# Two groups of four heads per TensorE step in a five-part cross-attention stack

## The chip, the cores and the metric

One of the eight cores of a Trainium2 chip runs the whole program. The metric is the device time of one execution in microseconds, the median over runs. A profiled execution gives the trace: a start and a duration for each instruction of TensorE (PE for its matmuls, PEld for its weight loads), VectorE (DVE), ScalarE (ACT), GpSimd (POOL) and of the DMA queue of SyncE (SP).

## What is computed

16 sequences of 128 tokens with 128 channels pass through five attentions (parts L0, L1, L2, L3S, L3C). L0 has 8 heads, the others 16 heads of 8 channels. Cut to what matters:

```python
x = x + attention(layernorm(x), layernorm(ctx), heads=8)                    # L0
x = x + attention(x, ctx, heads=16, mask=causal & key_padding)              # L1
x = x + attention(x, ctx, heads=16) @ Wo + bo                               # L2
x = x + gelu(x @ W1 + b1) @ W2 + b2
x = layer_norm(x + attention(x, x, heads=16, mask=causal * pad) @ Wo1 + bo1)      # L3S
x = layer_norm(x + attention(x, ctx, heads=16, mask=pad) @ Wo2 + bo2)             # L3C
x = layer_norm(x + gelu(x @ W1 + bf1) @ W2 + bf2)
# attention: softmax(q k^T / sqrt(head channels)) v for each head, with float32 results
```

## The kernel before

**Units and positions.** A unit is two sequences (b = 0, 1) of one part: 8 units a part, 40 in all. Each unit has 8 positions of its own (`SLOT`), and `schedule()` puts every step of every unit at a position, before or behind its own first one: projections about three units ahead (`PREPARE`), the scores one unit ahead (`SCORE_AT`), the feed-forward work up to four units behind (`CHAIN`). Within a position `RANK` sets the order. All five engines walk the one list `STEPS` in order and do their share of each step, with semaphores between them, so no engine overtakes in the list.

**A group** is four heads of one sequence. A unit of L1 to L3C has eight groups, one at each position; a unit of L0 has four, one at every second position. For each group:

- `score`: queries times keys, 128x512, to one of two banks `score_ps`. VectorE takes the negated row maxima from it (line 745, `score_reduced`). Only these are used of it. When the four groups of a sequence are done, `nmax` splits the maxima into bf16 terms, `n_tr` transposes them and SyncE writes them into the operand `pairs` (`max_landed`).
- `attn`: keys times queries, transposed, with the maxima as further contraction rows, to one of two banks `attn_ps`; ScalarE takes the exponential (line 645, `exp_done`) into a ring of 5 buffers `probs`. In L1 GpSimd then zeroes what lies ahead of the diagonal (step `causal`, line 533).
- `pv`: probabilities times values, into the one bank `o_ps`, one or two positions after `attn` (`PV_AFTER`). After a sequence's last `pv`, ScalarE copies the bank out (`o_evac`, `o_saved`), `o_tr` transposes it, VectorE divides it into `attn_tok`, and `a_tr` transposes that back.

**The shapes on TensorE.** Masks (`diagonal`, line 816) are four 32x32 tiles: 32 rows, 32 columns. The `score` and `attn` matmuls of 16 heads contract 52 or 55 rows that begin at partition 0 for even units and at 64 for odd ones, half of the rows each; from L1 on the `attn` of unit u and the `score` of unit u+1 are issued in turn, four pairs of them, and lie in the two halves of the array at once (call them pairs). `pv` uses all 128 rows and 32 columns a head, four heads beside each other; float32 is two passes, so a group has eight matmul records. All else (projections, transposes, feed-forward; the steps in `MISC`) uses the whole 128x128 array and writes three banks `misc_ps` in turn, which VectorE or ScalarE empties (`evacuated`). L1 masks its scores; L3S masks its scores and its `attn`; L2 and L3C mask nothing.

**The order at a position before.** `attn` has rank -2 and comes first, with its masks and pairs; the transposes and small projections follow; `pv` of two positions ago has rank 25; `a_tr`, `wo` and the feed-forward have rank 30. On VectorE the reduction (`score`) has rank 2. TensorE's waits ahead of a group's matmuls are: the group two before reduced (`score_reduced`), the group two before exponentiated (`exp_done`), and for the first of a sequence `max_landed`.

Of the kernel before, what the change touches and what calls it, by code (L numbers as in the profile page):

```python
# [31 lines left out]
P = 128  # L32
BATCHES, S, D, FF = 16, 128, 128, 512
PAIR = 2
# [14 lines left out]
PROBS_RING = 5  # L49
# [26 lines left out]
    L1: (("qk", -25), ("split", -25), ("rest", -24), ("term1", -23), ("term2", -22), ("v", -13)),  # L76
    L2: (("qk", -25), ("split", -25), ("rest", -24), ("term1", -23), ("term2", -22), ("v", -11)),
    L3S: (("qk", -25), ("split", -25), ("rest", -24), ("term1", -23), ("term2", -22), ("v", -14)),
    L3C: (("qk", -25), ("split", -25), ("rest", -24), ("term1", -23), ("term2", -22), ("v", -13)),
# [4 lines left out]
PV_AFTER = {L0: 1, L1: 2, L2: 2, L3S: 2, L3C: 2}  # L84
O_TR_AFTER = {L0: 1, L1: 1, L2: 1, L3S: 1, L3C: 1}
CHAIN = {
    L0: (("a_tr", 10),),
    L1: (("a_tr", 13),),
    L2: (("a_tr", 12), ("wo", 13), ("w1", 15), ("w1", 15), ("square", 17), ("square", 18), ("cube", 18),
         ("cube", 19), ("tanh", 21), ("tanh", 21), ("gelu", 21), ("gelu", 22), ("w2_first", 25), ("w2", 26)),  # L90
    L3S: (("a_tr", 11), ("wo", 13), ("x_tr", 16), ("x_stats", 18), ("x_norm", 19), ("x_back", 22)),
    L3C: (("a_tr", 11), ("wo", 13), ("x_tr", 14), ("x_stats", 15), ("x_norm", 17), ("x_back", 19), ("w1", 21),
          ("w1", 21), ("w2_first", 23), ("w2", 24), ("x_tr", 27), ("x_stats", 28), ("x_norm", 30), ("out", 30),
          ("store", 30)),
# [3 lines left out]
RANK = {"attn": -2, "causal": 4, "w2": 17, "score": 2, "nmax": 11, "n_tr": 15, "o_tr": 16, "load": 20, "ln_in": 20,  # L98
        "raw_tr": 20, "ln_norm": 14, "ln_tr": 2, "qk": 20, "split": 20, "rest": 20, "term1": 20, "term2": 20,
        "v": 20, "mask": 20, "stack": 20, "pv": 25, "o_evac": 2, "a_tr": 30, "wo": 30, "w1": 30, "square": 14,  # L100
# [14 lines left out]
def schedule():  # L115
# [6 lines left out]
    for u in range(UNITS):  # L122
        part = u // SETS
        quads = HEADS[part] // QUAD
        every = 4 // quads
# [4 lines left out]
        for b in range(PAIR):  # L130
            for g in range(quads):
                pos = 4 * b + every * g
# [5 lines left out]
            last = 4 * b + every * (quads - 1)  # L138
# [51 lines left out]
def build(nc, x, ctx_in, weights, cols, rows, valid, valid_t, pad, pad_t, out):  # L190
    with ExitStack() as stack:
# [55 lines left out]
        attn_tok = sb("attn_tok", [P, PAIR, D])  # L247
# [410 lines left out]
        def _(dve):  # L658
            for step in STEPS:
# [103 lines left out]
                if kind == "o_tr":  # L763
# [4 lines left out]
                    dst = attn_tok[:, b, :].rearrange("p (h e) -> p h e", e=d)  # L768
# [36 lines left out]
        def _(pe):  # L805
# [47 lines left out]

            for step in STEPS:
# [60 lines left out]
                if kind == "attn":  # L915
# [4 lines left out]
                    if beside:  # L920
                        score_begins(beside)
                    if g == 0:

                        pe.wait_ge(max_landed[m % 4], (m // 4 + 1) * 16)
# [135 lines left out]
```

## Time and profile before

| | us |
|---|---|
| median of 3 runs | 562.75 (554.84 to 569.61) |
| profiled execution | 558.87 |
| its span, first to last instruction | 557.1 |
| granted TensorE clock, mean | 0.932 |

The first `attn` group of each part is exponentiated at 42 us (L0), 131 us (L1), 233 us (L2), 334 us (L3S) and 432 us (L3C); the last group of all near 532 us. The clock column of a window is the share of 2.4 GHz that was granted in it on the mean; the clock has two levels, 1.2 and 2.4 GHz. Busy time of PE counts overlapping matmuls once and is modelled at its end, so the start times of successive matmuls tell more of its speed than its busy share does.

### The profile page before, as it was taken

The numbers are of one execution on the slowest core, as the hardware profiler recorded it, in microseconds if no ns is written. First come the engines' busy times: TensorE is split into PE (matmuls) and PEld (weight loads), VectorE is DVE, ScalarE is ACT, GpSimd is POOL, SyncE is SP. The second block draws the span as 40 slices with busy tenths as digits, with TensorE's granted clock in tenths as the row PEclk, the third lists the DMA queues.
The fourth block names the chain that finished last, engine by engine and source line by source line (L and its number), as shares of the span: only waits on it lengthen the run. The fifth ranks groups of instructions, "written<-read, shape, count | busy, mean of one in ns | idle before, by whom it ended". The sixth has DMA issues, their size and how long they took to land.

```text
span 557.1 us, 16733 instructions
## 1 busy us (share of the span) xinstructions
PE 486.3 (87%) x6464; PEld 299.2 (54%) x6464; DVE 407.6 (73%) x1093; ACT 329.0 (59%) x662; POOL 263.4 (47%) x334
## 2 busy tenths in 40 slices
PE   1548876799999878899999999999999999999973
PEld 1436554455555544455666666565555556666652
DVE  6267876645688886687888877778878897788452
ACT  1424655433556554467777766656666767888851
POOL 3585776824666774524344433334333533422243
PEclk9977889965799996799999999999999999999998
DMA  4593323332233332232223322232333332220000
GB/s 112 99 274 100 103 60 96 81 72 62 64 68 86 76 78 54 59 77 69 69 67 69 69 62 60 54 70 63 77 69 85 80 79 60 69 62 14 13 20 19
DMA packets 72021, 40.68 MB, mean 73 GB/s; under 512 B 7016, under 2 KB 71560, under 8 KB 71816
## 3 DMA queue, kind: packets, MB, share of 16 engines
q1 hardware_dynamic: 71944, 39.61, 30.1%
q8 instruction: 53, 0.87, 0.7%
q14 instruction: 24, 0.20, 0.1%
HBM read 5.00 MB, written 1.05 MB: 11 GB/s over the span
## 4 chain that ended last, share of the span: by engine, by line
PE 65%; POOL 9%; ACT 7%; DVE 6%; SPq 5%; issue 4%; DMA 3%; POOLq 0%; ACTq 0%; DVEq 0%
PE o_ps L963 14%; PE attn_ps L933 12%; PE misc_ps L993 5%; PE misc_ps L984 5%; PE misc_ps L895 5%; PE misc_ps L970 4%; PE misc_ps L901 4%; PE misc_ps L896 3%; PE score_ps L816 3%; PE misc_ps L980 2%; POOL probs L533 2%; PE misc_ps L976 2%; POOL rest L521 2%; PE misc_ps L912 2%; POOL terms L523 2%
## 5 line engine op out<-in xcount | busy, mean ns | idle before, releaser
L745 DVE TENSOR_REDUCE max_words<-score_ps 128x4 f32<-128x512 f32 x288 | 195.8, 685 | 67.7 <-PE score_ps L849 66.1
L645 ACT ACTIVATE probs<-attn_ps 128x512 f32<-128x512 f32 x288 | 169.8, 596 | 110.5 <-PE attn_ps L933 107.2
L963 PE MATMUL o_ps<-probs,v 128*32 128x128 f32 x2304 | 127.0, 294 | 12.6 <-POOL probs L533 8.0
L849 PE MATMUL score_ps<-pairs 52*128 52x128 bf16 (+1 forms) x1152 | 118.7, 226 | 9.1 <-DMA pairs<-terms 9.1
L521 POOL TENSOR_TENSOR rest<-qk_f,terms 128x512 f32<-128x512 f32 x40 | 46.2, 1155 | 162.3 <-ACT terms L596 162.3
L933 PE MATMUL attn_ps<-pairs 55*128 55x128 bf16 (+1 forms) x1152 | 117.8, 225 | 1.9 <-issue 1.0
L933 PEld LDWEIGHTS attn_ps<-pairs 55*128 55x128 bf16 (+1 forms) x1152 | 66.7, 97 | 49.9 <-issue 34.1
L963 PEld LDWEIGHTS o_ps<-probs,v 128*32 128x32 f32 x2304 | 46.3, 110 | 60.0 <-issue 16.9
L849 PEld LDWEIGHTS score_ps<-pairs 52*128 52x128 bf16 (+1 forms) x1152 | 69.8, 98 | 11.0 <-DMA pairs<-terms 9.5
L533 POOL TENSOR_SCALAR_AFFINE_SELECT probs<-probs 128x512 f32<-128x512 f32 x64 | 39.9, 635 | 22.4 <-ACT probs L645 22.4
L527 POOL TENSOR_TENSOR terms<-rest,terms 128x512 bf16<-128x512 f32 x40 | 46.8, 1170 | 1.9
L654 ACT ACTIVATE o_sb<-o_ps 128x256 f32<-128x256 f32 x80 | 30.9, 386 | 27.8 <-PE o_ps L963 27.6
L523 POOL TENSOR_TENSOR terms<-qk_f,terms 128x512 bf16<-128x512 f32 x40 | 46.1, 1153 | 0.0
L970 PE MATMUL misc_ps<-ident,o_sb 128*128 128x128 f32 x160 | 35.0, 302 | 9.8 <-ACT o_sb L654 9.0
L513 POOL TENSOR_SCALAR var_eps<-mean_var 128x2 f32<-128x2 f32 (+1 forms) x32 | 7.1, 222 | 75.7 <-DVE mean_var L682 75.7
L993 PE MATMUL misc_ps<-hidden,w 128*128 128x256 f32 x128 | 34.5, 396 | 1.0 <-ACT hidden L633 1.0
L755 DVE TENSOR_TENSOR max_words<-max_words 128x16 f32<-128x16 f32 (+1 forms) x80 | 31.6, 395 | 2.8
L784 DVE SCALAR_TENSOR_TENSOR xT<-misc_ps,col,xT 128x256 f32<-128x256 f32 x40 | 19.3, 482 | 18.9 <-PE misc_ps L980 13.9
L984 PE MATMUL misc_ps<-xT,w 128*128 128x256 f32 x128 | 31.8, 392 | 0.7 <-DVE xT L800 0.7
L584 ACT ACTIVATE qk_f<-misc_ps,col 128x256 f32<-128x256 f32 x24 | 11.4, 473 | 33.9 <-PE misc_ps L896 33.9
L816 PE MATMUL score_ps<-mask_l,ident_bf 32*32 32x128 bf16 x512 | 31.1, 233 | 0.0
L766 DVE RECIPROCAL recip<-misc_ps 128x16 f32<-128x16 f32 (+1 forms) x80 | 19.3, 241 | 13.9 <-PE misc_ps L970 13.4
(104 smaller groups left out, 766.8 us busy)
## 6 DMA issues: line engine op xcount, KB each, us to landing
pairs<-terms SPq DMA_DIRECT2D x240, 128.0 KB
w<-in_weights_dram SPq DMA_DIRECT2D x1, 1984.0 KB, 8.8
x_tok<-in_x_dram SPq DMA_DIRECT2D x8, 128.0 KB, 3.2
c_tok<-in_ctx_dram SPq DMA_DIRECT2D x8, 128.0 KB, 3.3
pairs<-max_rows SPq DMA_DIRECT2D x64, 12.0 KB
out_dram<-x_tok SPq DMA_DIRECT2D x8, 128.0 KB, 1.8
pairs<-constant_rows SPq DMA_DIRECT2D x4, 112.0 KB
row<-in_rows_dram SPq DMA_DIRECT2D x1, 320.0 KB, 4.4
```

The costliest lines, as they stand in the source:

```text
L521: pool.tensor_tensor(rest[:, :, :], qk_f32[:, :, :], terms[:, :, 0, :], ALU.subtract)
L523: pool.tensor_tensor(terms[:, :, 1, :], qk_f32[:, :, :], terms[:, :, 0, :], ALU.subtract)\
L533: pool.affine_select(out=probs[n % PROBS_RING][:, :, :], in_=probs[n % PROBS_RING][:, :, :], compare_op=ALU.is_ge, fill=0.0, base=0, patte ...
L645: act.activation(probs[n % PROBS_RING][:, :, :].rearrange("p h q -> p (h q)"), attn_ps[n % 2][:, :], ACT.Exp, scale=float(D // HEADS[part] ...
L745: dve.tensor_reduce(max_words[ub(step) % 2][:, QUAD * g:QUAD * (g + 1)], score_ps[n % 2][:, :].rearrange("p (h k) -> p h k", h=QUAD), AX_X ...
L816: pe.matmul(bank[part_, :].rearrange("p (h n) -> p h n", h=4)[:, :, part_], ident_bf[part_, part_], mask[part_, part_].unsqueeze(1).to_bro ...
L849: return pe.matmul(score_ps[NUM[step] % 2][:, j * S:(j + 1) * S], tile[score_rows(u), QUAD * g + j, 0, b * S:(b + 1) * S], tile[score_rows ...
L933: last = pe.matmul(attn_ps[n % 2][:, j * S:(j + 1) * S], pairs[attn_rows(u), h, 1, b * S:(b + 1) * S], pairs[attn_rows(u), h, 0, b * S:(b ...
L963: last = pe.matmul(o_ps[32 * j:32 * j + 32, region * P:(region + 1) * P], values, probs[n % PROBS_RING][:, j, :], start=part == L0 or g % ...
L970: last = pe.transpose(bank[:, k * P:(k + 1) * P], o_sb[ub(step) % 2][:, k * P:(k + 1) * P], ident[:, :])
L984: last = pe.matmul(bank[:, half * TOK:(half + 1) * TOK], weight(f"w1_{part}_{2 * b + half}"), xT[s][:, :], start=True, stop=True)
L993: last = pe.matmul(bank[:, 0:TOK], weight(f"w2_{part}_{c}"), hidden[:, c, :], start=(c == 0), stop=(c == 3))
```

## The change

- **Two groups at a position, every second position.** In L1 to L3C groups 2k and 2k+1 stand at one position (`together = 2`); L0 stays as it was.
- **One TensorE step for both**, in L1 and L3S, and where the unit beside is masked: the masks of both groups, then the sixteen pairs' matmuls. Both groups' waits then stand ahead of the first mask. In L2 and L3C the two groups stand one behind the other, each with its own waits.
- **`pv` right behind them** (rank 1 instead of 25, in L0 too), two groups together, two positions after their `attn`, four in L1. `score` gets rank 0 instead of 2: the two reductions come first on VectorE.
- **Other steps move** by one to four positions: projections in `PREPARE`, `o_tr` two positions behind the last `pv` instead of one, the chain so that most steps stand two positions behind what they need. The last chain ends at 33 instead of 30.
- **Buffers:** `probs` 6 instead of 5, `attn_tok` two instead of one.

No matmul, activation, reduction or DMA is added or taken away.

```diff
-PROBS_RING = 5
+PROBS_RING = 6
...
-    L1: (("qk", -25), ("split", -25), ("rest", -24), ("term1", -23), ("term2", -22), ("v", -13)),
-    L2: (("qk", -25), ("split", -25), ("rest", -24), ("term1", -23), ("term2", -22), ("v", -11)),
-    L3S: (("qk", -25), ("split", -25), ("rest", -24), ("term1", -23), ("term2", -22), ("v", -14)),
-    L3C: (("qk", -25), ("split", -25), ("rest", -24), ("term1", -23), ("term2", -22), ("v", -13)),
+    L1: (("qk", -24), ("split", -24), ("rest", -23), ("term1", -22), ("term2", -21), ("v", -11)),
+    L2: (("qk", -26), ("split", -26), ("rest", -25), ("term1", -24), ("term2", -23), ("v", -11)),
+    L3S: (("qk", -24), ("split", -24), ("rest", -23), ("term1", -22), ("term2", -21), ("v", -11)),
+    L3C: (("qk", -24), ("split", -24), ("rest", -23), ("term1", -22), ("term2", -21), ("v", -11)),
...
-PV_AFTER = {L0: 1, L1: 2, L2: 2, L3S: 2, L3C: 2}
-O_TR_AFTER = {L0: 1, L1: 1, L2: 1, L3S: 1, L3C: 1}
+PV_AFTER = {L0: 1, L1: 4, L2: 2, L3S: 2, L3C: 2}
+O_TR_AFTER = {L0: 1, L1: 2, L2: 2, L3S: 2, L3C: 2}
 CHAIN = {
     L0: (("a_tr", 10),),
-    L1: (("a_tr", 13),),
-    L2: (("a_tr", 12), ("wo", 13), ("w1", 15), ("w1", 15), ("square", 17), ("square", 18), ("cube", 18),
-         ("cube", 19), ("tanh", 21), ("tanh", 21), ("gelu", 21), ("gelu", 22), ("w2_first", 25), ("w2", 26)),
-    L3S: (("a_tr", 11), ("wo", 13), ("x_tr", 16), ("x_stats", 18), ("x_norm", 19), ("x_back", 22)),
-    L3C: (("a_tr", 11), ("wo", 13), ("x_tr", 14), ("x_stats", 15), ("x_norm", 17), ("x_back", 19), ("w1", 21),
-          ("w1", 21), ("w2_first", 23), ("w2", 24), ("x_tr", 27), ("x_stats", 28), ("x_norm", 30), ("out", 30),
-          ("store", 30)),
+    L1: (("a_tr", 14),),
+    L2: (("a_tr", 12), ("wo", 14), ("w1", 16), ("w1", 18), ("square", 17), ("square", 19), ("cube", 18),
+         ("cube", 20), ("tanh", 19), ("tanh", 21), ("gelu", 20), ("gelu", 22), ("w2_first", 24), ("w2", 26)),
+    L3S: (("a_tr", 12), ("wo", 14), ("x_tr", 16), ("x_stats", 17), ("x_norm", 18), ("x_back", 20)),
+    L3C: (("a_tr", 12), ("wo", 14), ("x_tr", 16), ("x_stats", 17), ("x_norm", 18), ("x_back", 20), ("w1", 22),
+          ("w1", 22), ("w2_first", 26), ("w2", 28), ("x_tr", 30), ("x_stats", 31), ("x_norm", 32), ("out", 33),
+          ("store", 33)),
...
-RANK = {"attn": -2, "causal": 4, "w2": 17, "score": 2, "nmax": 11, "n_tr": 15, "o_tr": 16, "load": 20, "ln_in": 20,
+RANK = {"attn": -2, "causal": 4, "w2": 17, "score": 0, "nmax": 11, "n_tr": 15, "o_tr": 16, "load": 20, "ln_in": 20,
...
-        "v": 20, "mask": 20, "stack": 20, "pv": 25, "o_evac": 2, "a_tr": 30, "wo": 30, "w1": 30, "square": 14,
+        "v": 20, "mask": 20, "stack": 20, "pv": 1, "o_evac": 2, "a_tr": 30, "wo": 30, "w1": 30, "square": 14,
...
-        every = 4 // quads
+        together = 2 if part > L0 else 1
+        every = 4 * together // quads
...
-                pos = 4 * b + every * g
+                pos = 4 * b + every * (g // together)
...
-            last = 4 * b + every * (quads - 1)
+            last = 4 * b + every * (quads // together - 1)
...
+            def attn_begins(step):
+
+                u = step.u
+                n, m = NUM[step], ub(step)
+                if beside(step):
+                    score_begins(beside(step))
+                if step.g == 0:
+
+                    pe.wait_ge(max_landed[m % 4], (m // 4 + 1) * 16)
+                if n >= 2:
+
+                    pe.wait_ge(exp_done, n - 1)
+                if u // SETS == L3S:
+                    diagonal(attn_ps[n % 2], mask_l3_t)
+
+            def attn_matmuls(step):
+
+                kind, u, b, g = step
+                part = u // SETS
+                n = NUM[step]
+                pairs, base = stack_of(u)
+                for j in range(QUAD):
+                    h = head_of(part, g, j)
+                    last = pe.matmul(attn_ps[n % 2][:, j * S:(j + 1) * S],
+                                     pairs[attn_rows(u), h, 1, b * S:(b + 1) * S],
+                                     pairs[attn_rows(u), h, 0, b * S:(b + 1) * S],
+                                     start=part != L3S, stop=True, skip_group_check=True)
+                    if beside(step):
+                        last_score = score_matmul(beside(step), j)
+                last.then_inc(attn_ready, 1)
+                if beside(step):
+                    last_score.then_inc(score_ready, 1)
...
+                    two_at_once = score_mask(step) is not None or score_mask(the("score", u + 1, b, g)) is not None
+                    if part == L0 or not two_at_once:
+                        attn_begins(step)
+                        attn_matmuls(step)
+                    elif g % 2 == 0:
+                        odd = the("attn", u, b, g + 1)
+                        attn_begins(step)
+                        attn_begins(odd)
+                        attn_matmuls(step)
+                        attn_matmuls(odd)
...
```

## Rows read from the trace of the kernel before

**Rows 1.** The page: busy time and share of the span of each engine.
```profile
PE 486.3 (87%) x6464; PEld 299.2 (54%) x6464; DVE 407.6 (73%) x1093; ACT 329.0 (59%) x662; POOL 263.4 (47%) x334
```

**Rows 2.** Windows by stage: stretch, length, busy us (count) per engine, clock, DMA.
```profile
core 0: us, PE busy (x) PEld busy (x) DVE busy (x) ACT busy (x) POOL busy (x), PEclk, DMA share, GB/s
42.30:85.70 43.40, 35.12 (x348) 24.88 (x348) 34.66 (x114) 23.23 (x53) 29.50 (x36) 0.82 0.33 85
...
157.20:180.10 22.90, 20.32 (x356) 11.63 (x352) 19.84 (x43) 13.03 (x27) 16.48 (x22) 1.00 0.34 75
...
203.10:233.30 30.20, 25.89 (x325) 14.09 (x323) 19.95 (x44) 13.19 (x28) 16.49 (x22) 0.72 0.29 67
...
280.20:306.40 26.20, 26.20 (x328) 16.23 (x326) 23.22 (x53) 18.75 (x39) 10.99 (x11) 1.00 0.28 66
...
385.90:408.90 23.00, 22.91 (x433) 13.36 (x429) 18.48 (x53) 15.25 (x31) 8.72 (x10) 1.00 0.30 68
...
481.10:507.60 26.50, 25.76 (x329) 16.13 (x328) 21.79 (x64) 21.14 (x41) 9.25 (x14) 1.00 0.22 58
...
533.00:557.10 24.10, 12.02 (x69) 8.19 (x67) 9.72 (x37) 6.83 (x16) 8.96 (x16) 0.90 0.08 22
```

**Rows 3.** Timeline of PE in L2: start us, length us, line, output and inputs.
```profile
287.14 0.70 PE L980 MATMUL misc_ps<-attnT,w 128*128 128x256 f32 x2
287.77 0.23 PE L933 MATMUL attn_ps<-pairs 55*128 55x128 bf16 x1
...
287.83 0.22 PE L933 MATMUL attn_ps<-pairs 55*128 55x128 bf16 x1
...
287.95 0.22 PE L933 MATMUL attn_ps<-pairs 55*128 55x128 bf16 x1
...
288.10 0.44 PE L970 MATMUL misc_ps<-ident,o_sb 128*128 128x128 f32 x2
288.46 0.43 PE L963 MATMUL o_ps<-probs,v 128*32 128x128 f32 x8
288.82 0.23 PE L933 MATMUL attn_ps<-pairs 55*128 55x128 bf16 x1
```

**Rows 4.** Timeline in L3S: the masks of scores and attn, then the pairs.
```profile
396.47 0.23 PE L816 MATMUL score_ps<-mask_l,ident_bf 32*32 32x128 bf16 x4
...
396.54 0.22 PE L816 MATMUL attn_ps<-mask_l_t,ident_bf 32*32 32x128 bf16 x4
...
396.69 0.09 PEld L933 LDWEIGHTS attn_ps<-pairs 55*128 55x128 bf16 x1
```

**Rows 5.** Timeline of PE at the end of the attention work.
```profile
533.38 0.64 PE L963 MATMUL o_ps<-probs,v 128*32 128x128 f32 x16
```

**Rows 6.** Timeline of PE in L1: two projections with nothing between.
```profile
166.01 0.70 PE L895 MATMUL misc_ps<-xT,w 128*128 128x256 f32 x2
166.55 0.59 PE L896 MATMUL misc_ps<-cT,w 128*128 128x256 f32 x2
```

**Rows 7.** Timeline in L1: first pair of a group, then exponential and reduction.
```profile
171.15 0.23 PE L933 MATMUL attn_ps<-pairs 55*128 55x128 bf16 x1
...
171.58 0.60 ACT L645 ACTIVATE probs<-attn_ps 128x512 f32<-128x512 f32 x1 [1.09 <-PE attn_ps L933]
171.61 0.69 DVE L745 TENSOR_REDUCE max_words<-score_ps 128x4 f32<-128x512 f32 x1 [0.39 <-PE score_ps L849]
```

**Rows 8.** Waits in L2, 280.2 to 306.4: total us, times, longest us.
```profile
PEld attn_ps L933 <- DVE max_words L745: 0.7, 2, 0.3
PEld o_ps L963 <- ACT probs L645: 0.7, 2, 0.3
```

**Rows 9.** Waits in L1, 157.2 to 180.1, same columns.
```profile
PEld o_ps L963 <- POOL probs L533: 3.2, 6, 1.0
```

**Rows 10.** Waits of the whole span, same columns.
```profile
PEld score_ps L849 <- DMA pairs<-terms: 9.5, 2, 5.7
```

More of the change, by code:

```diff
@@ L246, in build @@
         recip = sb("recip", [P, 16])
-        attn_tok = sb("attn_tok", [P, PAIR, D])
+        attn_tok = [sb(f"attn_tok{r}", [P, PAIR, D]) for r in range(2)]
         attnT = sb("attnT", [P, TOK])
@@ L767, in _ @@
                     dve.wait_ge(recip_done, ub(step) + 1)
-                    dst = attn_tok[:, b, :].rearrange("p (h e) -> p h e", e=d)
+                    dst = attn_tok[u % 2][:, b, :].rearrange("p (h e) -> p h e", e=d)
                     spread = recip[:, 0:heads].unsqueeze(2).to_broadcast([P, heads, d])
@@ L852, in score_matmul, with beside @@
                                  start=score_mask(step) is None, stop=True, skip_group_check=True)
+            def beside(step):
+                u = step.u
+                return the("score", u + 1, step.b, step.g) if u // SETS > L0 and u + 1 < UNITS else None
+            def attn_begins(step):
+                u = step.u
+                n, m = NUM[step], ub(step)
[23 more added lines that the diff above has]
+                    last_score.then_inc(score_ready, 1)
             for step in STEPS:
@@ L858, in _ @@
                 d = D // heads
-                pairs, base = stack_of(u)
                 if kind in MISC and kind != "w2":
@@ L915, in _ @@
                 if kind == "attn":
-                    n, m = NUM[step], ub(step)
-                    beside = the("score", u + 1, b, g) if part > L0 and u + 1 < UNITS else None
[L920 to L924, printed above, removed]
-                    if n >= 2:
-                        pe.wait_ge(exp_done, n - 1)
-                    mask = {L3S: mask_l3_t}.get(part)
-                    if mask is not None:
-                        diagonal(attn_ps[n % 2], mask)
-                    for j in range(QUAD):
-                        h = head_of(part, g, j)
-                        last = pe.matmul(attn_ps[n % 2][:, j * S:(j + 1) * S],
-                                         pairs[attn_rows(u), h, 1, b * S:(b + 1) * S],
-                                         pairs[attn_rows(u), h, 0, b * S:(b + 1) * S],
-                                         start=mask is None, stop=True, skip_group_check=True)
-                        if beside:
-                            last_score = score_matmul(beside, j)
-                    last.then_inc(attn_ready, 1)
-                    if beside:
-                        last_score.then_inc(score_ready, 1)
+                    two_at_once = score_mask(step) is not None or score_mask(the("score", u + 1, b, g)) is not None
[8 more added lines that the diff above has]
+                        attn_matmuls(odd)
                 if kind == "pv":
@@ L975, in _ @@
                     for k in range(PAIR):
-                        last = pe.transpose(bank[:, k * P:(k + 1) * P], attn_tok[:, k, :], ident[:, :])
+                        last = pe.transpose(bank[:, k * P:(k + 1) * P], attn_tok[u % 2][:, k, :], ident[:, :])
                     last.then_inc(misc_ready, 1)
```

## The prediction

> **What bounds the kernel now.** I read the page's busy shares first. PE leads with 87%, DVE follows with 73%, then ACT and POOL [rows 1]. A share over the whole span mixes the parts, so next I cut the span into windows that hold two units each. In L2 PE is busy for all of 26.20 us and DVE for 23.22; in L3S it is 22.91 and 18.48 of 23.00; in L3C 25.76 and 21.79 of 26.50, with ACT at 21.14; in L1 20.32 and 19.84 of 22.90 [rows 2]. Since busy PE is a modelled figure, I checked it by the waits: in 26.2 us of L2 TensorE's weight loads waited 0.7 us for a reduction and 0.7 us for an exponential [rows 8]. So from 233 us on TensorE issues almost without a stop, and its order sets the time. In L1 two units also held 3.2 us of waits of `pv` for GpSimd's causal step [rows 9]; the unit there takes 11.45 us, and TensorE is not alone in setting it. The rest is L0 to 131 us, which the change hardly touches, and the tail from 533 us.
>
> **What TensorE spends between shapes.** The timeline gives starts. Two pairs in a row start 0.06 us apart (287.77, 287.83), but what follows the last pair (287.95) starts 0.15 us behind it (288.10): a change of shape costs 0.09 us [rows 3]. The same shows elsewhere: two 256-column float32 matmuls take 0.54 us when a full-array matmul follows [rows 6] and 0.63 us when pairs follow (287.14 to 287.77) [rows 3]. Masks behind masks cost 0.07 us, and pairs behind masks 0.15 [rows 4]. A `pv` group takes 0.36 us from its start to the next shape's (288.46 to 288.82) [rows 3]. Two `pv` groups in a row occur once: 16 records last 0.64 us where 8 last 0.43 [rows 5, 3], so the second adds 0.21 and a join saves 0.15.
>
> **What the change takes away.** I counted changes of shape along the list of steps, an issue order and no time. L3S shows the pattern: before, each of a unit's eight groups went misc, masks, pairs, misc, `pv` (32 or 33 changes a unit); after, each of four steps goes masks, pairs, `pv`, misc (16). Over the eight units, counted up to the next part's first `attn`: L1 236 to 114, L2 203 to 99, L3S 260 to 128, L3C 209 to 98. L0 keeps 165 (164). That is 469 fewer, times 0.09 = 42 us, and 128 joined `pv` groups save 0.15 - 0.09 = 0.06 us more each, 8 us. TensorE alone would give 50 us.
>
> **What takes part of it back.** No work leaves the other engines, so DVE becomes the next bound. Per unit:
> - L1: DVE is busy 9.92 us of 11.45 [rows 2]. TensorE would need about 11.45 - 1.6 (its halved `pv` waits) - 122/8 x 0.09 - 0.24 = 8.2. DVE decides. Also, two of the four steps hold little or no misc. Both groups' waits stand ahead of the masks there, so the loop shows: masks 0.07 + 0.15 [rows 4], first pair to first reduction 0.46, two reductions of 0.69 [rows 7] make 2.06, against TensorE's own 0.22 + 0.57 + 0.57 = 1.36 (two groups of pairs; two of `pv`). The two sparse steps lose 0.7 and about 0.3 us, which fits inside DVE's 9.92. I take 10.3, 1.15 less.
> - L2: 13.10 - 13 x 0.09 - 0.24 = 11.7 for TensorE, 11.6 for DVE. With two engines so near each other and one list, neither is ever full; I take 12.1, 1.0 less.
> - L3S: 11.50 - 16.5 x 0.09 - 0.24 = 9.8, DVE 9.2. The step with only `o_tr` (0.36) loses 0.3: masks 3 x 0.07 + 0.15 = 0.36, + 0.46 + 1.38 = 2.20 against 0.36 + 0.57 + 0.57 + 0.36 = 1.86. I take 10.3, 1.2 less.
> - L3C: 13.25 - 13.9 x 0.09 - 0.24 = 11.8, DVE 10.9, ACT 10.6. I take 12.2, 1.0 less for seven units.
>
> **Moved steps.** `pv` at rank 1 no longer has misc ahead of it. In L1 to L3C it reads exponentials that the pairs ahead of it waited for, so it costs nothing; if they were late it would be the pairs that wait. In L1 four positions, half a unit or some 5 us, stand between `attn` and `pv`, and GpSimd is busy for 8.2 us a unit [rows 2], so it keeps up; if this cover went, the 1.6 us a unit of today's waits would come back, 13 us in L1. In L0 `pv` may wait for its exponential instead of following a projection: from first pair to exponential 0.43, and 0.60 for it [rows 7], less the scores issued between, at most 0.6 us a group, 32 groups, 19 us. Against that, `o_evac` comes earlier, which could give back some of PE's idle time, 8 us of 43 up to 86 us [rows 2]. L0's PE is idle often enough to hide it; I take 0, and -4 to +5 for the range. `n_tr` and its write of the maxima now stand four positions ahead of the `attn` that reads them instead of three, about 5 us. On SP, behind `n_tr` wait the stack writes of a later unit; their landing is awaited seven positions on as before, and TensorE waited for such a landing only twice in the span [rows 10]. Two `attn_tok` and six `probs` only take waits away. Tail: the last chain goes from 30 to 33, so a `w2`, an `x_tr` and their norms of the unit before, and the store of the one before that, move past the last group, where nothing covers them. The tail now is 24.1 us for 25 positions, 12 us of it PE [rows 2]. Three positions at the mean would be 2.9 us, nothing if it stayed hidden; I take +2.5.
>
> **The sum.** L1 8 x 1.15 = 9.2, L2 8 x 1.0 = 8.0, L3S 8 x 1.2 = 9.6, L3C 7 x 1.0 = 7.0, tail -2.5: 31.3 us off the profiled execution's 558.87, so 527.6, or 5.6%. The median of the runs is 0.7% above that execution; 5.6% off 562.75 is 531.
>
> **The rivals.**
> - *DVE holds the loop, the gain is small.* For it: DVE at 89% in L2, reductions now in blocks of 1.38 us ahead of the evacuations, and three `misc_ps` banks, so that a step's fourth misc waits. Against it: the waits of L2 show DVE holding TensorE for 0.7 us in 26. If each of the 124 steps of two groups lost 0.3 us more, 37 us would eat the whole saving: 568. With half of that, 0.15 us a step, 550. Same. The Trainium skill (Perfetto Trace Analysis, Identifying the Most-Contended Engine) would judge TensorE's distance from its limit by weight-load busy share instead of matmul share, and others by occupancy. By it DVE (73%) leads TensorE (54%) [rows 1], and TensorE's savings bring nothing: 563. The two-unit windows speak against it, since TensorE stood still only where it changed shape.
> - *The clock falls (slower).* TensorE was granted 1.2 GHz through most of the two units from 203 us, which took 30.20 us against 22.90 for two units of the same work at 2.4 GHz: 3.65 us a unit. Just before it fell the units ran as those at 157 us, so L1 stands near the edge. In L1 and L3S the merged step leaves both banks full and TensorE idle up to 0.7 us at a time. If that brought 1.2 GHz to the five clear units of L1 and all of L3S: 13 x 3.65 = 47 us, less the 31: 579, slower. From nine such units on nothing is gained, from twelve on it is slower by 2%. The Trainium skill (TensorE: Matmul & The Clock Gate, A second HAM failure mode: psum-queue depth-cycling) tells of such a kernel, whose clock swings while it cycles PSUM banks; no run here shows that yet. Against it: the same matmuls come in less time, and L2 to L3C ran wholly at 2.4.
> - *The clock holds in L1.* The three slow units (45 us in all) then fall to 10.3: another 10 us beyond the sum, 521, and with each part down to the larger of its two sums (9.9, 11.7, 9.8, 11.8) another 13, 508.
> - *The joins save nothing.* Pairs of a second group write another bank and `pv` adds to the same one. If a second group paid 0.15 as a new shape does: 128 joins of pairs at 0.09 and 128 of `pv` at 0.15 fall out of the 50 us, 19 stay, and less the tail 546. The row with 16 records speaks against it for `pv`.
>
> **Chances.** The forecast (517 to 545) 0.64; the clock holds 0.13; DVE holds the loop 0.13; the clock falls 0.07; no joins 0.03. Two percent, about what a measurement of this kernel can tell from no change, is 551.5 to 574. Faster 0.81: forecast, held clock, no joins and 0.01 of DVE's case. Same 0.13: the rest of DVE's case and 0.01 of the clock's. Slower 0.06. The range of 8 in 10 leaves out half of the held clock's case and of DVE's and all of the falling clock's, 0.2 in all: 510, near the lowest sum, to 550, DVE's milder price.
>
> **What would show it.** Right: two-unit windows of about 24.2 us in L2, 20.6 in L3S and L1 and 24.4 in L3C; PV rows of x16 at 0.64; in the waits of L1 no GpSimd row for `pv`, but masks waiting for reductions. Wrong: windows of L2 above 25.5, TensorE waiting more than 1 us a unit for DVE; a clock under 1.00 behind 234 us; a tail over 30 us.

## The result and the profile after

The changed kernel takes 636.8 us (median of four runs, 631.3 to 642.2) against 564.1 us: a ratio of 1.136, 95% interval 1.110 to 1.162. The forecast was 531, with 510 to 550 as its range. The profiled execution took 639.55 us, with a span of 637.8 and a granted clock of 0.836. Executions of one kernel differ by some per cent, mostly with the clock that they are granted, and the profiled ones of e8, e9, e14 and e16 are among the slower of theirs (549.0 us against a median of 542.7 in e9, 619.3 against 607.6 in e14).

The two windows views below cut both traces at the first exponential of each part. Columns: stretch, length, busy us (and count) of PE, PEld, DVE, ACT, POOL, mean granted clock, DMA share, GB/s. The lines are L1, L2, L3S, L3C and the tail. First the kernel before:

```profile
130.80:233.30 102.50, 91.74 (x1369) 51.09 (x1369) 78.17 (x168) 52.58 (x105) 65.99 (x88) 0.84 0.30 68
233.30:333.60 100.30, 97.58 (x1294) 60.11 (x1293) 82.38 (x193) 72.38 (x151) 41.24 (x38) 1.00 0.29 67
333.60:431.90 98.30, 98.02 (x1702) 58.33 (x1698) 76.83 (x206) 63.91 (x127) 35.30 (x39) 1.00 0.30 69
431.90:532.40 100.50, 96.60 (x1231) 59.62 (x1230) 78.06 (x230) 78.70 (x152) 36.00 (x51) 1.00 0.22 52
532.40:557.10 24.70, 12.62 (x71) 8.72 (x69) 10.16 (x38) 7.43 (x17) 9.41 (x17) 0.91 0.08 22
```

Then the changed kernel:

```profile
130.50:232.50 102.00, 82.57 (x1365) 56.81 (x1360) 77.94 (x168) 51.53 (x106) 65.41 (x88) 0.83 0.32 70
232.50:340.70 108.20, 91.38 (x1298) 64.69 (x1299) 85.72 (x192) 66.38 (x144) 41.17 (x36) 0.94 0.26 61
340.70:468.10 127.40, 108.29 (x1703) 72.18 (x1698) 87.47 (x208) 61.19 (x130) 38.03 (x40) 0.82 0.24 56
468.10:599.00 130.90, 105.51 (x1223) 71.40 (x1219) 80.34 (x221) 74.49 (x146) 34.09 (x47) 0.80 0.17 41
599.00:637.80 38.80, 20.36 (x102) 14.40 (x90) 12.13 (x47) 9.64 (x23) 11.32 (x20) 0.81 0.05 14
```

Three things are to be seen. TensorE's idle time (length less PE busy) went from 10.8, 2.7, 0.3, 3.9 and 12.1 us to 19.4, 16.8, 19.1, 25.4 and 18.4: 69 us more in all, while the whole grew by 81. The clock, which stayed at 2.4 GHz from 233 us to the tail before, falls again and again, so that the same matmuls keep TensorE busy for 108.3 us in L3S instead of 98.0. And in L3S VectorE is busy for 87.5 us instead of 76.8 with the same instructions. L0 is unchanged, as expected (130.5 us against 130.8).

Where TensorE's new idle time comes from shows in the waits of the changed kernel (total us, times, longest us):

```profile
DVE stats L679 <- ACT x_rows L616: 30.7, 16, 3.3
PE misc_ps L1027 <- DVE normed L722: 19.2, 11, 4.4
PEld attn_ps L883 <- DVE max_words L746: 16.7, 18, 1.6
PE score_ps L817 <- DMA pairs<-max_rows: 14.9, 8, 3.4
```

The same four waits in the kernel before:

```profile
DVE stats L678 <- ACT x_rows L615: 3.6, 5, 1.3
PE misc_ps L1005 <- DVE normed L721: 2.9, 5, 1.5
PEld attn_ps L933 <- DVE max_words L745: 3.9, 12, 0.6
PE attn_ps L933 <- DMA pairs<-max_rows: 0.2, 1, 0.2
```

Added up by what TensorE's matmuls waited for, before and after: exponentials (`probs` from ScalarE) 3.6 and 21.7 us, `normed` 2.9 and 19.2, reductions 0.7 and 18.9, the landing of the maxima 0.2 and 16.7, `attn_tok` nothing and 11.9; the waits for GpSimd's causal step, 8.0 us before, are gone. So there is no single wait that holds the loss.

One step of L3S shows the first and the third (timeline, changed kernel; start us, length us):

```profile
454.38 0.38 PE L1021 MATMUL misc_ps<-ident,xT 128*128 128x128 f32 x2
...
454.69 0.29 PE L817 MATMUL attn_ps<-mask_l_t,ident_bf 32*32 32x128 bf16 x8
...
455.46 0.64 PE L985 MATMUL o_ps<-probs,v 128*32 128x128 f32 x16
455.80 0.37 ACT L616 ACTIVATE x_rows<-misc_ps 128x256 f32<-128x256 f32 x1
...
456.20 0.48 DVE L679 BATCH_NORM_STATS2 stats<-x_rows 128x6 f32<-128x128 f32 x2 [2.21 <-ACT x_rows L616]
...
456.88 1.25 DVE L746 TENSOR_REDUCE max_words<-score_ps 128x4 f32<-128x512 f32 x2
...
457.60 0.23 PE L817 MATMUL attn_ps<-mask_l_t,ident_bf 32*32 32x128 bf16 x4 [1.12 <-DVE max_words L746]
...
458.19 0.23 PE L817 MATMUL attn_ps<-mask_l_t,ident_bf 32*32 32x128 bf16 x4 [0.36 <-DVE max_words L746]
```

The transpose `x_tr` (454.38) stands at position 16, the statistics at 17, the next joined pairs at 18. Position 17 holds no pairs, so "one position behind" means directly behind. VectorE stood for 2.21 us at the statistics, because ScalarE had the projections' copies ahead of `x_rows`. The scores of the first group were ready near 455.4 (their first pair started at 454.91, and [rows 7] has 0.46 us from there to a reduction), but the reductions started only at 456.88, 1.5 us later. TensorE, which had issued all it had by 456.5, waited for the first until 457.60 and for the second until 458.19.

### The profile page after: what moved, and what is told of

Read it like the earlier page. It is cut to its first block, busy times and chain, and to the rows that moved or that the text cites. A ratio compares the mean times of both kernels' runs of the same rounds, so it can differ in the third digit from the quotient of the medians.

```text
span 637.8 us, 16746 instructions
## 1 busy us (share of the span) xinstructions
PE 494.0 (77%) x6464; PEld 340.6 (53%) x6464; DVE 424.1 (67%) x1093; ACT 316.5 (50%) x660; POOL 265.6 (42%) x334
## 4 chain that ended last, share of the span: by engine, by line
PE 45%; DVE 28%; DMA 7%; issue 6%; ACT 6%; POOL 4%; SPq 3%; ACTq 0%; POOLq 0%; DVEq 0%
DVE max_words L746 11%; PE attn_ps L883 8%; PE o_ps L985 8%; DMA pairs<-max_rows 5%; PE misc_ps L1015 5%; DVE max_words L756 4%; PE misc_ps L939 4%; PE misc_ps L1006 3%; PE misc_ps L933 3%; PE misc_ps L992 3%; DVE max_words L759 2%; PE misc_ps L934 2%; DVE normed L722 2%; DVE gelu_arg L791 2%; PE score_ps L817 2%
## 5 line engine op out<-in xcount | busy, mean ns | idle before, releaser
L746 DVE TENSOR_REDUCE max_words<-score_ps 128x4 f32<-128x512 f32 x288 | 185.6, 680 | 82.7 <-PE score_ps L850 81.7
L646 ACT ACTIVATE probs<-attn_ps 128x512 f32<-128x512 f32 x288 | 158.0, 595 | 126.9 <-PE attn_ps L883 126.6
L883 PE MATMUL attn_ps<-pairs 55*128 55x128 bf16 (+1 forms) x1152 | 108.2, 238 | 22.2 <-DVE max_words L746 8.8
L985 PE MATMUL o_ps<-probs,v 128*32 128x128 f32 x2304 | 111.5, 314 | 14.0 <-ACT probs L646 14.0
L883 PEld LDWEIGHTS attn_ps<-pairs 55*128 55x128 bf16 (+1 forms) x1152 | 75.7, 104 | 56.1 <-issue 30.6
L850 PEld LDWEIGHTS score_ps<-pairs 52*128 52x128 bf16 (+1 forms) x1152 | 78.3, 105 | 12.0 <-DMA pairs<-terms 10.2
L985 PEld LDWEIGHTS o_ps<-probs,v 128*32 128x32 f32 x2304 | 60.2, 120 | 37.1 <-ACT probs L646 16.8
L1015 PE MATMUL misc_ps<-hidden,w 128*128 128x256 f32 x128 | 41.9, 459 | 19.1 <-DVE attn_tok L779 11.6
L534 POOL TENSOR_SCALAR_AFFINE_SELECT probs<-probs 128x512 f32<-128x512 f32 x64 | 39.0, 638 | 21.8 <-ACT probs L646 21.7
L817 PE MATMUL score_ps<-mask_l,ident_bf 32*32 32x128 bf16 x512 | 26.8, 240 | 23.9 <-DMA pairs<-max_rows 14.9
L756 DVE TENSOR_TENSOR max_words<-max_words 128x16 f32<-128x16 f32 (+1 forms) x80 | 41.1, 514 | 2.8
L540 POOL TENSOR_TENSOR gelu_arg<-half_h 128x512 f32<-128x512 f32 x16 | 18.4, 1147 | 52.6 <-ACT half_h L631 52.4
L1015 PEld LDWEIGHTS misc_ps<-hidden,w 128*128 128x128 f32 x128 | 25.7, 222 | 26.2 <-DVE attn_tok L779 12.6
L785 DVE SCALAR_TENSOR_TENSOR xT<-misc_ps,col,xT 128x256 f32<-128x256 f32 x40 | 19.2, 480 | 26.5 <-PE misc_ps L1002 16.8
```

The lines of the kernel that those rows point to most:

```text
L646: act.activation(probs[n % PROBS_RING][:, :, :].rearrange("p h q -> p (h q)"), attn_ps[n % 2][:, :], ACT.Exp, scale=float(D // HEADS[part] ...
L746: dve.tensor_reduce(max_words[ub(step) % 2][:, QUAD * g:QUAD * (g + 1)], score_ps[n % 2][:, :].rearrange("p (h k) -> p h k", h=QUAD), AX_X ...
L756: dve.tensor_tensor(second, first, upper_half(words, 0, heads), ALU.subtract)\
L850: return pe.matmul(score_ps[NUM[step] % 2][:, j * S:(j + 1) * S], tile[score_rows(u), QUAD * g + j, 0, b * S:(b + 1) * S], tile[score_rows ...
L883: last = pe.matmul(attn_ps[n % 2][:, j * S:(j + 1) * S], pairs[attn_rows(u), h, 1, b * S:(b + 1) * S], pairs[attn_rows(u), h, 0, b * S:(b ...
L985: last = pe.matmul(o_ps[32 * j:32 * j + 32, region * P:(region + 1) * P], values, probs[n % PROBS_RING][:, j, :], start=part == L0 or g % ...
```

## The experiments

All are compared with the kernel before, which ran beside them at medians of 557 to 564 us. The numbers are medians of device time. The variants ran on several occasions, so a difference of a few us between two of them that did not run beside each other is not safe; where it matters the ratio to the kernel before is given.

### Which part of the change costs

**e1, one group at a position, the rest as changed.**

```diff
-        together = 2 if part > L0 else 1
+        together = 1
-PV_AFTER = {L0: 1, L1: 4, ...}
+PV_AFTER = {L0: 1, L1: 3, ...}
```

`w2_first` also stands one position later in L2 and L3C, and the merged step is taken apart as in e2.

> One group at a position again in L1 to L3C; the positions of the other steps, the ranks and the buffers stay as changed (pv of L1 three positions behind instead of four, w2_first one ahead of w2, since groups no longer pair up). Loop theory (two groups at once leave the reductions of a step between VectorE's other work and TensorE's next step): near the kernel before, 560 to 585 us. Moves theory (the new positions and ranks cost the time): 615 to 640 us. Clock theory (the clock falls with pv and projections in blocks): clock 0.85 as after.

Measured 675.5 us, clock 0.827: slower than the whole change, and above both of its ranges. The loop theory falls as a theory of the whole loss. With groups standing singly the moved steps and the ranks cost 115 us, but part of that is e1's own: the last `pv` of a sequence stands one position later than in the change, so `o_tr` of the second one stands at 11 in L2 to L3C, directly ahead of `a_tr` at 12, and TensorE waits at `a_tr` for `attn_tok`. The wait of the statistics for `x_rows`, with both at the positions of the change, is nearly gone, since position 17 holds pairs here (waits):

```profile
PE misc_ps L998 <- DVE attn_tok L779: 22.7, 19, 2.0
DVE stats L679 <- ACT x_rows L616: 2.7, 4, 1.3
```

What the rest of e1's loss is was not broken down.

**e2, the merged step taken apart.** `if part == L0 or not two_at_once:` becomes `if True:`.

> Groups still two at a position, but the merged step is undone: each group of L1 and L3S has its own waits, masks and matmuls. Merged-waits theory (both banks must be free before the first mask): L1 and L3S come back by 2 us a unit, 600 to 610 us. Loop theory: the second group waits for the same reductions, so 625 to 640 us.

Measured 635.3 us against 636.8, as the loop theory expected. Merging the waits of two groups costs nothing of note.

**e3, all other steps at their positions of before** (`PREPARE`, `PV_AFTER`, `O_TR_AFTER`, `CHAIN` from the kernel before; grouping and ranks as changed).

> Grouping, ranks and buffers as changed; all other steps at the positions of the kernel before (projections, o_tr, pv of L1, chain). Moves theory: 560 to 590 us. Loop theory: no better than the change, 620 to 660 us, since it is the grouping that costs.

Measured 589.0 us, 48 less than the change. The tail is back at 25.7 us.

**e5, only the grouping** (e3 with `pv` at rank 25 and `score` at 2).

> Two groups at a position, masks and pairs of both together, and nothing else of the change: positions of all other steps and ranks as before (so pv stands behind the transposes again), buffers as changed. e3 took 589 us with the new ranks. Ranks theory (pv ahead of the transposes makes all that follows them late): 540 to 565 us, at or below the kernel before. Loop theory (the grouping itself costs): 580 to 600 us.

Measured 595.5 us, ratio 1.068 (1.060 to 1.077). With e3, the new ranks are worth 6 us to the grouped kernel.

**e6, only the ranks** (kernel before with `pv` at 1, `score` at 0).

> The kernel before with only the ranks of pv (25 to 1) and score (2 to 0) changed: one group at a position, pv directly behind the pairs. Ranks theory: 580 to 620 us. If the new chain positions carry the cost: 560 to 568 us.

Measured 567.7 us, ratio 1.019 (1.010 to 1.028), at the upper end of the second expectation. From L2 on its parts take 99.2, 98.5 and 101.1 us, as before; the difference lies in L1, 114.5 us at a mean clock of 0.69 instead of 102.5 at 0.84. So what `pv` ahead of the transposes costs, if anything, is the clock in L1.

**e7, only the chain at its old positions.**

> The changed kernel with only the chain behind the attention (a_tr, wo, feed-forward, norms) at its old positions; projections, o_tr, pv of L1 and ranks as changed. Chain theory (steps that stand one odd position behind their producer hold up VectorE and TensorE): near e3, 585 to 600 us. If projections or o_tr carry the cost: 620 to 640 us.

Measured 612.7 us, ratio 1.096 (1.084 to 1.108): between the two expectations: 24 less than the change, 24 more than e3, which also has the old projections, `v`, `o_tr` and `pv` of L1. The moves do not simply add up. The wait of the statistics falls to 5.1 us, but with `o_tr` at 10 and `a_tr` back at 11 in L3S and L3C TensorE waits for `attn_tok` instead, 31.1 us against 12.2 in e10 below, which has the same distance but the old projections, `v` and `pv` of L1:

```profile
PE misc_ps L998 <- DVE attn_tok L779: 31.1, 20, 2.7
```

The tail is 25.5 us, so the changed tail is all the chain's.

**e8, only the ranks as before.** `"pv": 25`, `"score": 2` in the changed kernel.

> The changed kernel with only the ranks of pv and score as before. Ranks theory: 580 to 600 us, and together with the old positions (e5) below the kernel before. Chain theory: 615 to 640 us.

Measured 648.0 us, 11 more and above both expectations. Here too the new ranks help the grouped kernel; they are not the cause.

**e10, e3 with `o_tr` two positions behind `pv`** (`O_TR_AFTER` as changed).

> As e3 (grouping, new ranks, old positions), but o_tr two positions behind the last pv as in the change. In e3 TensorE waited 44 us in 57 places for ScalarE's copy of the pv bank ahead of o_tr. If that round trip was on the path: 550 to 570 us. If the time is set elsewhere: 580 to 592 us. Against e7 (613 us) it differs by the projections' new positions and L1's late pv alone: if these cost by VectorE waiting for GpSimd's splits, VectorE's busy time is back from about 88 to 77 us a part.

Measured 580.9 us, ratio 1.048 (1.039 to 1.057), at the lower edge of the second expectation. Of e3's 44 us of waiting ahead of `o_tr` 8 came back; most of it was not on the path. This is the best form found with joined pairs and the old chain. Its L3S (windows view) shows the forecast's mechanism and its loss side by side:

```profile
343.30:445.00 101.70, 88.88 (x1706) 61.05 (x1698) 77.55 (x207) 59.16 (x127) 35.66 (x39) 0.98 0.29 66
```

TensorE is busy for 9.1 us less than before (98.0), and idle for 12.5 us more (12.8 against 0.3).

### The chain: whole steps

**e12, the norms of the chain one whole step behind each producer.** L3C's feed-forward and its second norm move back with them, and two waits keep the statistics of two units apart.

```diff
-    L3S: (... ("x_tr", 16), ("x_stats", 17), ("x_norm", 18), ("x_back", 20)),
+    L3S: (... ("x_tr", 16), ("x_stats", 18), ("x_norm", 20), ("x_back", 22)),
-    L3C: (... ("x_stats", 17), ("x_norm", 18), ("x_back", 20), ("w1", 22), ("w1", 22), ("w2_first", 26),
-          ("w2", 28), ("x_tr", 30), ("x_stats", 31), ("x_norm", 32), ("out", 33), ("store", 33)),
+    L3C: (... ("x_stats", 18), ("x_norm", 20), ("x_back", 22), ("w1", 24), ("w1", 24), ("w2_first", 29),
+          ("w2", 30), ("x_tr", 34), ("x_stats", 36), ("x_norm", 38), ("out", 39), ("store", 39)),
```

> The changed kernel with norms in the chain one whole step (two positions) behind each producer: statistics two positions behind their transpose, normalisation two behind those, instead of one and one; the last chain ends at 39. Two waits are added between statistics of two units. Odd-position theory (statistics at an odd position stand in the same step as the transpose they wait for, ahead of the next reductions): VectorE's wait for x_rows goes from 31 us to under 8, L3S and L3C fall by 1 to 2 us a unit, 605 to 625 us, with a tail of 40 us or more. If that wait was covered: 635 to 650 us.

Measured 594.0 us, ratio 1.072 (1.063 to 1.082): 43 less than the change, by moving steps further back. VectorE's wait for `x_rows` (waits) and the parts L3S, L3C (windows):

```profile
DVE stats L683 <- ACT x_rows L618: 6.2, 4, 2.5
```

```profile
334.80:439.60 104.80, 92.35 (x1702) 64.15 (x1696) 86.35 (x204) 60.86 (x131) 37.73 (x40) 0.95 0.28 65
439.60:557.40 117.80, 95.70 (x1205) 67.96 (x1203) 76.74 (x222) 73.90 (x145) 32.50 (x45) 0.85 0.20 47
```

The wait went from 30.7 to 6.2 us, L3S from 127.4 to 104.8 and its clock from 0.82 to 0.95. More than that wait came back. With the norms and `x_back` moved too, TensorE's own waits for `normed` fell from 19.2 to 2.9 us and those for `attn_tok` from 11.9 to about 1, while those for the landing of the maxima rose from 16.7 to 30.2. And of the 22.6 us that L3S lost, 15.9 are TensorE's busy time for the same matmuls (108.3 to 92.4), at the higher clock, and 6.7 are idle time. How much the position of the statistics brings by itself was not run.

### The projections: VectorE behind GpSimd

**e13, e12 with the projections' positions of before** (`qk`, `split`, `rest`, `term1`, `term2`; `v` as changed).

> e12 (594 us) with qk, split, rest, term1 and term2 of L1 to L3C at their positions before, v as changed. Contention theory (GpSimd's splits now run while VectorE splits the maxima, whose 0.2 us then take 1.1): VectorE's busy time falls from 86 to 78 us in L2 and L3S, and the time to 570 to 582 us. If the projections' positions do not matter: 588 to 600 us.

Measured 586.0 us, ratio 1.041 (1.036 to 1.047), between the two expectations. VectorE's busy time in L3S went from 86.4 to 78.2 us, and the part from 104.8 to 100.0; in L1 it went from 78.1 to 71.6, and the part from 102.0 to 95.2. In L2 it stayed at 86.6, and the part took 6.0 us more. So the theory holds for L3S and L1, not for L2. The gain is 8 us by the medians, and 17 by the ratios, since the kernel before ran at 557.1 us beside e12 and at 562.4 beside e13.

What the theory rests on is in the trace of the changed kernel (timeline in L3S and L2, VectorE and GpSimd):

```profile
458.08 1.16 POOL L524 TENSOR_TENSOR terms<-qk_f,terms 128x512 bf16<-128x512 f32 x1
458.17 1.10 DVE L756 TENSOR_TENSOR max_words<-max_words 128x16 f32<-128x16 f32 x1
459.31 0.17 DVE L759 TENSOR_TENSOR max_words<-max_words 128x16 f32<-128x16 f32 x1
```

```profile
318.27 1.16 POOL L522 TENSOR_TENSOR rest<-qk_f,terms 128x512 f32<-128x512 f32 x1
318.38 1.08 DVE L759 TENSOR_TENSOR max_words<-max_words 128x16 f32<-128x16 f32 x1
```

The instruction that splits the maxima takes 0.17 us alone and 1.08 to 1.10 us where a GpSimd split had begun 0.1 us before it: it ends when that one ends. The Trainium skill (SBUF — State Buffer, SBUF: two separate sides) says that VectorE and GpSimd share one pair of SBUF ports as an exclusive lock, held for a whole instruction, when the VectorE one has two SBUF inputs and the GpSimd one reads SBUF; the traces agree, and the reductions, which read PSUM, kept their 0.68 us. By line, the two splits of the maxima cost 31.6 and 21.2 us before, 41.1 and 29.7 after.

### Who sets the time: TensorE before, the round trip after

**e4 and e16, row maxima over 64 of 128 keys,** in the changed kernel and in the kernel before; **e17,** in e10.

```diff
-                                      score_ps[n % 2][:, :].rearrange("p (h k) -> p h k", h=QUAD),
+                                      score_ps[n % 2][:, :].rearrange("p (h k) -> p h k", h=QUAD)[:, :, 0:64],
```

> The changed kernel with each row maximum taken over the first 64 of 128 keys: a reduction takes about 0.35 us instead of 0.68. The maximum is then over half of the keys. If the reductions stand in the loop: 288 x 0.33 = 95 us less at most, 550 to 590 us, and the clock back above 0.9. If TensorE's own order or its clock sets the time: above 620 us.

> The kernel before with each row maximum taken over the first 64 of 128 keys (e4 did this to the change and took 28 us off). If TensorE's issue bounds the kernel before and reductions are hidden: 550 to 562 us, within 2%. If the reductions are in the loop there too: 530 to 545 us.

> e10 (581 us) with each row maximum taken over 64 of 128 keys. A joined step waits for the reductions of the step before, and for its exponentials. If the reductions are what TensorE waits for: 15 to 30 us less, 550 to 566 us, against 4 us in the kernel before (e16). If it is the exponentials, the transposes or the clock: 572 to 582 us.

Measured 609.5 us in the changed kernel (27 less), 558.0 in the kernel before (4 less, ratio 0.988, 0.983 to 0.992) and 563.3 in e10 (18 less, ratio 1.016, 1.000 to 1.032). The halved instruction, 0.42 us instead of 0.68, saves VectorE about 75 us in each. Before, nearly all of it was hidden behind TensorE. With joined pairs a part is on the path. In the changed kernel the gain lies between the two expectations; that VectorE often stands at a wait there, which a shorter reduction only lengthens, was argued and not tested.

That reductions are on the path does not mean that TensorE stands waiting for them. In e10 its matmuls waited for them for 4.6 us in all (0.7 before), and much longer for exponentials and for `attn_tok`, which VectorE writes behind its reductions (waits of e10):

```profile
PE misc_ps L998 <- DVE attn_tok L779: 12.2, 11, 1.4
PE o_ps L985 <- ACT probs L646: 11.1, 14, 1.5
PE attn_ps L883 <- ACT probs L646: 6.6, 12, 1.4
PE score_ps L817 <- DVE max_words L746: 2.9, 9, 0.7
```

In all, waits for `attn_tok` rose from nothing to 18.7 us and those for exponentials from 3.6 to 20.3. With halved reductions (e17) `attn_tok` fell to 12.5, and the exponentials' wait stayed at 20.3. This points to what stands behind the longer blocks on VectorE, more than to the next pairs; no run parts the two.

**e11 and e14, the transposes `o_tr`, `a_tr`, `x_tr`, `x_back` issued three times** with the same data, in the changed kernel and in the kernel before.

```diff
-                    for k in range(2):
+                    for k in 3 * [0, 1]:
```

> The changed kernel with each of the transposes o_tr, a_tr, x_tr and x_back issued three times instead of once, same data, same bank; 0.4 us more of TensorE work for each. Clock theory (the low clock is a large part of the loss): the clock goes above 0.90 and the time falls or stays, 610 to 640 us. If the low clock only follows the waits: clock below 0.87 and 640 to 680 us.

> The kernel before with o_tr, a_tr, x_tr and x_back issued three times, as e11 did to the change (there 637 became 632 us). About 190 steps with 4 more matmuls of 0.11 us, 75 to 85 us of TensorE work. If TensorE's issue bounds the kernel before: 600 to 635 us. If it had spare time as after the change: under 580 us.

Measured 632.5 us for the changed kernel (4 less than without) and 607.6 for the kernel before (ratio 1.076, 1.067 to 1.085: 45 more). L3S in windows, first e11, then e14:

```profile
335.90:455.20 119.30, 105.60 (x1848) 78.51 (x1842) 87.19 (x208) 60.82 (x130) 38.05 (x40) 0.99 0.26 58
```

```profile
358.00:472.10 114.10, 113.82 (x1851) 74.12 (x1843) 79.17 (x206) 64.70 (x127) 35.44 (x39) 1.00 0.26 60
```

Before, the added work lengthened L3S by 15.8 us, with 0.3 us of idle time: TensorE's issue is the bound. From L2 to L3C together the parts took 43 us more for 45 us more busy time. In the changed kernel the same work shortened L3S by 8.1 us, since the busier engine was granted 0.99 instead of 0.82. So the low clock seems to cost something there, of the order of those 8 us. This rests on one trace of each: in e2's trace, with nearly the same order of work, L3S took 124.0 us at 0.89, and the 4 us between the medians are within the spread of the changed kernel. But at nearly full clock and with more to do TensorE was still idle for 13.7 us of the part: the waits are not the clock's doing.

### What of the change pays

**e9, only `pv` joined.** The kernel before; the `pv` of an even group moves one position back, `probs` has 6 buffers. Pairs, reductions and exponentials stay at one group a position.

```diff
-                put(pos + PV_AFTER[part], Step("pv", u, b, g))
+                put(pos + PV_AFTER[part] + (part > L0 and g % 2 == 0), Step("pv", u, b, g))
```

> The kernel before; only the pv of an even group moves one position back, so that two pv groups follow each other, and probs has 6 buffers. Pairs, reductions and exponentials keep one group a position. If a join is worth what the row with 16 records shows (0.14 us, 128 of them) and nothing waits longer: 18 us less plus a few changes of shape with the transposes, 535 to 550 us, clock as before. If any grouping costs: 565 us or more.

Measured 542.7 us, ratio 0.977 (0.970 to 0.985). TensorE in L3S (timeline), and the whole of L3S (windows):

```profile
381.05 0.65 PE L963 MATMUL o_ps<-probs,v 128*32 128x128 f32 x16
381.62 0.70 PE L980 MATMUL misc_ps<-attnT,w 128*128 128x256 f32 x2
```

```profile
324.60:419.20 94.60, 93.60 (x1698) 60.22 (x1696) 77.72 (x206) 63.64 (x128) 35.24 (x39) 1.00 0.30 71
```

L3S takes 3.7 us less with 32 joins, 0.12 us each, near the 0.15 of [rows 3, 5]. L2 and L3C did not gain (101.7 and 100.5 us): TensorE is idle for 8.4 and 7.4 us there instead of 2.7 and 3.9, and in L2 VectorE is busy for 87.7 us, so the joins' gain went into the same waits. The rest of the gain is L1, 89.5 instead of 102.5 us, at a clock of 0.92 instead of 0.84; how much of that is chance in the clock was not settled.

**e15, e9 with `pv` of L1 one position later** and 8 buffers.

> e9 (543 us) with pv of L1 one position later and 8 buffers of probs: in e9 and before pv of L1 waits for GpSimd's causal step. If that wait is on the path at full clock: 533 to 541 us. If L1 is held by the clock and by VectorE: 541 to 548 us.

Measured 540.2 us, ratio 0.959 (0.953 to 0.966) to its own runs of before. It is the fastest kernel here. The waits of `pv`'s weight loads for GpSimd fell from 10.9 us in e9 to 0.4, and L1 took 83.0 us (windows):

```profile
129.00:212.00 83.00, 72.92 (x1349) 47.22 (x1346) 69.61 (x167) 53.73 (x104) 65.44 (x88) 0.98 0.37 84
```

## Why the prediction was wrong

- **"What bounds the kernel now" held.** TensorE's issue: from L2 to L3C e14 adds 45 us of work and gets 43 of them as time, e16 takes 75 us of VectorE's work away and gets 4.
- **"What TensorE spends between shapes" held.** Two joined `pv` groups last 0.64 us, as in [rows 5]. Of the 50 us of saving for TensorE alone, e10 shows 9.1 us of busy time in L3S where the forecast had 13.8, and e9 shows 3.7 us of time there by the `pv` joins alone, so "the joins save nothing" falls. For the other parts the clock differs too much between the traces to tell.
- **"What takes part of it back" failed.** I took each part's time as the larger of two busy sums plus a few tenths. But VectorE was never full: in L3S of the changed kernel it is busy for 87.5 of 127.4 us. What counts is when each result arrives. With two groups at a step, the next pairs need the reductions of the step directly before, and these stand in VectorE's list behind all it was given from that step's end. Before, a whole group lay between ([rows 8]: 0.7 us of waiting in two units). TensorE's matmuls waited for reductions for 0.7 us before and for 18.9 after. The loop that I summed (2.20 us against 1.86) assumed that VectorE stands free when the scores arrive; in the step shown above it came 1.5 us late. With the other steps at their old places (`o_tr` excepted in e10), joined groups cost 24, 29 and 38 us against the kernel before beside them (e10, e3, e5) instead of saving the 34 that the sum had for the four parts; with halved reductions e10 is 18 us faster. But the loop of reductions is not the whole step that failed: in e10 it holds TensorE itself for 4.6 us only, and the waits that grew are those for exponentials and for `attn_tok`, to which the prediction gave no time.
- **"Moved steps", put at nothing but the tail, was the largest miss.** They cost 48 us (e3), the tail among them. I counted distance in positions, but a position without pairs leaves little to do between producer and consumer; once groups stand at even positions, a consumer one odd position behind its producer has no cover. The statistics show it: at the same two positions VectorE waited 30.7 us with paired groups and 2.7 with single ones (e1). I looked at `pv`, `n_tr` and the queues, and not at `x_stats`, where VectorE now stood for 31 us ahead of its reductions. e12 gives 43 us back by moving the norms and what follows them to whole steps. Nor did I look at what runs on GpSimd while VectorE works: the moved projections put its splits on top of VectorE's two-input instructions, 17 us more busy time on VectorE over the span, and 8 to 17 us of time by e13. The 32 us between e7 and e10 hold the projections, `v` and `pv` of L1 together; `v` and `pv` of L1 were not moved alone.
- **The tail** was put at +2.5 us and is +14.1 (24.7 to 38.8). By e7 it is the chain. Its matmul records went from 71 to 102: more of the last units' feed-forward falls behind the last group than three positions at the mean. TensorE's busy time there grew by 7.7 us, its idle time by 6.4.
- **`n_tr`, "four positions instead of three, about 5 us"**, was right in steps and short in what stood ahead on the queue. In L1 (changed kernel, timeline) SyncE issues the maxima behind four stack writes:

```profile
165.47 3.23 SPq L428 DMA_DIRECT2D pairs<-terms  x4
...
168.53 0.24 PE L950 MATMUL misc_ps<-ident_bf,max_words 128*48 128x128 bf16 x1
...
169.58 0.76 SPq L444 DMA_DIRECT2D pairs<-max_rows  x1
...
173.95 0.23 PE L817 MATMUL score_ps<-mask_l,ident_bf 32*32 32x128 bf16 x4 [2.35 <-DMA pairs<-max_rows]
```

  The mask that waited for them started 4.4 us after their issue. TensorE had one more step to do meanwhile and waited for 2.35 us; in L1 this came in 8 places, 14.9 us in all, more than the 8.0 us of waits for GpSimd that went. This would explain why L1 gained nothing, and no run tests it. That the stack writes ahead make the landing late was argued from the order of issue, not tested either.
- **The rivals.** "The clock falls" named the right sign and the right symptom, with 7%. But the merged step, in which it saw the reason, was not the cause: e2 takes it apart, and the time stays; and the clock comes back when the waits go (e12: 0.82 to 0.95 in L3S) or when the waiting is filled with work (e11). In L3S the low clock goes with the idle time and adds to the loss: the same matmuls kept TensorE busy for 108.3 us there and for 88.9 in e10 at 0.98, 19 us more, of which the runs do not say how much is on the path. "DVE holds the loop" came nearest in mechanism, but at its dearest price of 0.3 us a step it gave 568.

Of the signs of being wrong, a window above 25.5 us for two units of L2 (27.05 at the mean), a clock under 1.00 behind 234 us and a tail over 30 us all came.

What stays open: how e10's 24 us divide between reductions, exponentials, `attn_tok` and the clock, how the 48 us of the moves divide between the single steps, what else costs e1 its time, and how much of e9's gain in L1 is its own.

## What to carry to other kernels

Where engines walk one ordered list, a step's distance from its producer is to be counted in work that stands between them on the consumer's engine, not in places of the list; grouping empties places that used to be cover. Before joining work on the bounding engine, write down for each other engine what it must finish between two joined steps and when its inputs arrive, in order; a comparison of busy sums does not see it. And join first what has nobody waiting on its double buffer (`pv` here: 14 us gained in e9, 22 in e15 with the later `pv` of L1), not what two engines feed back into the next step (the pairs: with them joined too, 24 to 38 us lost).

## What the runs showed of the hardware

- In L3S TensorE's granted clock went with its idle time both ways: it ran at 1.00 with 0.3 us idle in 98, at 0.82 with 19 in 127, and at 0.99 with 14 in 119 when 145 more matmuls filled it. With the added work that part was 8 us shorter in the one trace of it. Idle time alone does not tell the clock: L1 ran at 0.69 with 8.9 us idle in 114.5 (e6) and at 0.98 with 10.1 in 83.0 (e15).
- A VectorE instruction of 0.17 us with two SBUF inputs took 1.08 and 1.10 us where a GpSimd elementwise instruction of 1.16 us had begun 0.1 us before it, and ended 0.03 us after it.
